# A state-space block with a feed-forward layer on one core: engine orders, scan steps, transfers and the PSUM ring re-ordered

## The reference, cut to what matters

```python
# x: 8 batches x 1024 tokens x 512, fp32
x = L0_attn_x
x = x + _layernorm(_L0_attn_ref(_layernorm(x), ...))
x = x + _layernorm(_L0_ffn_ref(_layernorm(x), ...))

# _L0_attn_ref
s = sigmoid(silu(x @ s_w1.T + s_b1) @ s_w2.T + s_b2)      # 512 -> 256 -> 128
u = (x @ B_w.T + B_b) * s
h = h @ A.T + u_t                                         # scan over 1024 tokens, state 128
y = hs @ C_w.T + C_b + x @ D_w.T + D_b
return y * sigmoid(x @ g_w.T + g_b)

# _L0_ffn_ref: a shared expert, and routed experts whose weight is trunc(softmax of two)
out_shared = square(relu(xf @ Ws1)) @ Ws2                 # 512 -> 256 -> 512
```

## Time and profile before

| | |
|---|---|
| median of 3 runs | 957.19 us (956.58 to 958.75) |
| the profiled execution | 963.26 us, span 961.5 us |
| TensorE busy, of the span | 91% |
| VectorE, GpSimd, ScalarE busy | 58%, 45%, 32% |
| mean granted clock of TensorE | 0.974 |
| moved by transfers | 72.9 MB |

### The profile page before, as it was taken

One profiled execution on the slowest core, in us unless ns is written; L12 is line 12 of the kernel. 1 busy time (PEld: TensorE's weight loads), 2 busy tenths in 40 slices (PEclk: granted clock), 3 DMA queues, 4 the chain that ended last, 5 costly groups with the idle time before them and its releaser, 6 DMA issues. The chain is left out here.

```text
span 961.5 us, 13116 instructions
## 1 busy us (share of the span) xinstructions
PE 873.0 (91%) x4120; PEld 712.5 (74%) x4120; DVE 559.8 (58%) x1392; ACT 310.2 (32%) x530; POOL 435.6 (45%) x537
## 2 busy tenths in 40 slices
PE   5689999999889998899998998899988999899975
PEld 4577877788767887678776887678876788787764
DVE  4826764577536675377744776367762767534652
ACT  3331433233322333224332243322342233322232
POOL 1342455254534446254552554444452545615454
PEclk9889999999999999999999999999999999999987
DMA  9030102321140111421023211402114110122112
GB/s 302 5 141 35 45 1 93 127 89 44 45 176 19 69 44 44 176 87 44 0 81 138 88 44 44 162 14 88 44 44 176 44 71 16 44 88 88 45 44 89
DMA packets 15129, 72.91 MB, mean 76 GB/s; under 512 B 2403, under 2 KB 4835, under 8 KB 7014
## 3 DMA queue, kind: packets, MB, share of 16 engines
q1 hardware_dynamic: 15078, 72.38, 19.9%
HBM read 38.82 MB, written 33.55 MB: 75 GB/s over the span
## 5 line engine op out<-in xcount | busy, mean ns | idle before, releaser
L415 PE MATMUL TM<-gw_hi,xT_hi 128*128 128x512 f32 x256 | 106.4, 416 | 0.9 <-ACT apt L766 0.7
L1399 POOL TENSOR_TENSOR rsv<-rsv,negh 128x1 f32<-128x1 f32 x64 | 35.9, 561 | 154.6 <-DVE rsv L1082 154.6
L415 PE MATMUL TM<-dw_hi,xT_hi 128*128 128x512 f32 x256 | 102.5, 400 | 0.0
L839 ACT ACTIVATE work<-TM,nmz,rsz 128x512 f32<-128x512 f32 x62 | 48.3, 779 | 164.3 <-POOL nmz L1409 164.3
L417 PE MATMUL TM<-gw_hi,xT_lo 128*128 128x512 f32 x256 | 100.8, 394 | 0.0
L417 PE MATMUL TM<-dw_hi,xT_lo 128*128 128x512 f32 x256 | 100.4, 392 | 0.0
L416 PE MATMUL TM<-gw_lo,xT_hi 128*128 128x512 f32 x256 | 100.0, 391 | 0.0
L416 PE MATMUL TM<-dw_lo,xT_hi 128*128 128x512 f32 x256 | 99.7, 390 | 0.0
L778 ACT ACTIVATE work<-TM 128x512 f32<-128x512 f32 x64 | 38.4, 600 | 171.5 <-PE TM L417 102.6
L1078 DVE TENSOR_TENSOR work<-TM,work 128x512 f32<-128x512 f32 x64 | 44.1, 689 | 81.8 <-PE TM L417 81.8
L1450 POOL TENSOR_TENSOR h_lo<-hf,h_hi 128x512 fp32r<-128x512 f32 x32 | 42.6, 1333 | 108.2 <-DVE h_hi L1140 108.2
(11 more groups left out here) (145 smaller groups left out, 2156.6 us busy)
## 6 DMA issues: line engine op xcount, KB each, us to landing
xin<-in_x SPq DMA_DIRECT2D x16, 1024.0 KB, 7.8
xres<-in_x SPq DMA_DIRECT2D x16, 1024.0 KB, 7.0
x_scratch<-xres SPq DMA_DIRECT2D x16, 1024.0 KB, 3.9
out<-work SPq DMA_DIRECT2D x15, 1024.0 KB, 4.8
xres<-in_g_w_t SPq DMA_DIRECT2D x1, 1024.0 KB, 7.7
xres<-in_D_w_t SPq DMA_DIRECT2D x1, 1024.0 KB, 7.5
work<-in_Ws SPq DMA_DIRECT2D x2, 512.0 KB, 9.2
out<-work SPq DMA_DIRECT2D x4, 256.0 KB, 2.0
```

The source lines that it names most:

```text
L415: eng.matmul(ps, lhs[0], rhs[0], start=first, stop=False)
L839: eng.activation(work[:, j, :], z_bank(rep, j)[:, :], ACT.Identity, bias=nmz[:, j:j + 1], scale=rsz[:, j:j + 1]).then_inc(S["zn_ok"], 1)
L1399: return eng.tensor_tensor(dst, src, negh[:, 0:n], ALU.pow)
```

## The change

The work is the same but for small pieces; its order changes on all engines. On TensorE, scan steps go between groups of three products of W1f and G, two groups apart; G(2) and G(3) move ahead in the tail, and the TM ring with them; in the body W1f(0,1) moves before Y(7), FT(5) before SG(0), W2(0) before T(4), H(1,0) and H(1,1) before W2(2) and W2(3). The other engines' orders follow. On VectorE the column of ones in xin is written once for four tiles. On SP the store of the result is issued in quarters of a batch (two tiles each, four semaphores), and xin is loaded two batches ahead, each half after the FT that reads the last tile of it, ahead of the store of x1. SP's loop has one pass less. Left out below: the two new semaphores and the waits at the very end.

```diff
--- before.py
+++ after.py
@@ -210,7 +211,7 @@
-        TM_RING = (3, ["g0", "g1", "z4", "z5", "g2", "z6", "z7", "g3", "y0", "g4", "y1", "g5", "y2", "g6", "y3", "g7",
+        TM_RING = (3, ["g0", "g1", "g2", "z4", "z5", "g3", "z6", "z7", "y0", "g4", "y1", "g5", "y2", "g6", "y3", "g7",
                        "y4", "y5", "y6", "y7", "z0", "z1", "z2", "z3"])
@@ -342,12 +343,16 @@
+            def store_out(b, h):
+                js = slice(2 * h, 2 * h + 2)
+                eng.wait_ge(S["out_ok"], body_at("out_ok", b, 2 * h + 1))
+                eng.dma_start(out_v[b][:, js, :], work[:, js, :]).then_inc(S[f"out_st{h}"], 16)
+            def load_next_x(n, m):
+                eng.wait_ge(S["ft_done"], prep_at("ft_done", n - 1, m * MS + MS - 1))
+                load_x(n, m)
             def one_pass(b, rep):
-                if rep + 1 < NB:
-                    eng.wait_ge(S["ft_done"], prep_at("ft_done", b, L - 1))
-                    for m in range(NM):
-                        load_x(b + 1, m)
                 if rep == 0:
@@ -355,25 +360,26 @@
                         if m == NM - 1:
-                            eng.wait_ge(S["out_ok"], body_at("out_ok", b - 1, L - 1))
-                            eng.dma_start(out_v[b - 1][:, js, :], work[:, js, :]).then_inc(S[f"out_st{m}"], 16)
+                            store_out(b - 1, 2)
+                            store_out(b - 1, 3)
                         eng.wait_ge(S["x1_st" + str(m)], body_at("x1_st" + str(m), b - 1))
-                        if m < NM - 1:
-                            eng.wait_ge(S["out_ok"], body_at("out_ok", b - 1, m * MS + MS - 1))
+                        eng.wait_ge(S["out_ok"], body_at("out_ok", b - 1, m * MS + MS - 1))
                     eng.dma_start(xres[:, js, :], x_v[b][:, js, :]).then_inc(S[f"xres_ld{m}"], 16)
...
                     js = slice(m * MS, (m + 1) * MS)
+                    if rep + 2 < NB:
+                        load_next_x(b + 2, m)
                     eng.wait_ge(S["x1_ok"], body_at("x1_ok", b, m * MS + MS - 1))
                     eng.dma_start(x1_v[b][:, js, :], xres[:, js, :]).then_inc(S[f"x1_st{m}"], 16)
-                for m in range(NM - 1):
-                    js = slice(m * MS, (m + 1) * MS)
-                    eng.wait_ge(S["out_ok"], body_at("out_ok", b, m * MS + MS - 1))
-                    eng.dma_start(out_v[b][:, js, :], work[:, js, :]).then_inc(S[f"out_st{m}"], 16)
+                store_out(b, 0)
+                store_out(b, 1)
+            for m in range(NM):
+                load_next_x(1, m)
             one_pass(0, 0)
-            with eng.Fori(1, NB - 1) as b:
+            with eng.Fori(1, NB - 2) as b:
                 one_pass(b, 1)
+            one_pass(NB - 2, NB - 2)
             one_pass(NB - 1, NB - 1)
@@ -491,7 +497,7 @@
-            def W1f(b, rep, m, f):
+            def W1f(b, rep, m, f, steps={}):
@@ -503,7 +509,10 @@
                             (x2T_hi[:, :, k, :], x2T_lo[:, :, k, :]), k == 0, k == KD - 1)
-                r.then_inc(S["w1_done"], 1)
+                    if k == KD - 1:
+                        r.then_inc(S["w1_done"], 1)
+                    if k in steps:
+                        scan_step(b, rep, steps[k])
@@ -575,22 +584,18 @@
                     return
-                G(*a, 0, {2: 0, 3: 1})
-                W1f(*a, 1, 0)
-                scan_step(*a, 2)
-                W1f(*a, 1, 1)
-                scan_step(*a, 3)
-                G(*a, 1, {2: 4, 3: 5})
-                scan_step(*a, 6)
+                G(*a, 0, {2: 0})
+                W1f(*a, 1, 0, {0: 1, 2: 2})
+                W1f(*a, 1, 1, {0: 3, 2: 4})
+                G(*a, 1, {0: 5, 2: 6})
+                G(*a, 2, {0: 7, 2: 8})
                 W2(*a, 4)
-                scan_step(*a, 7)
+                scan_step(*a, 9)
                 W2(*a, 5)
-                G(*a, 2, {2: 8, 3: 9})
+                scan_step(*a, 10)
+                G(*a, 3, {1: 11})
                 W2(*a, 6)
-                scan_step(*a, 10)
                 W2(*a, 7)
-                scan_step(*a, 11)
-                G(*a, 3)
@@ -623,30 +628,29 @@
                     B(*a, 0)
+                    FT(*a, 5)
                     SG(*a, 0)
                 Y(*a, 6)
-                if prep:
-                    FT(*a, 5)
                 W1f(*a, 0, 0)
-                Y(*a, 7)
-                if prep:
+                if prep:
+                    W1f(*a, 0, 1)
+                    Y(*a, 7)
                     FT(*a, 6)
-                if prep:
-                    W1f(*a, 0, 1)
                     FT(*a, 7)
+                    W2(*a, 0)
                     T(*a, 4)
-                    W2(*a, 0)
                     W2(*a, 1)
                     T(*a, 5)
+                    H(*a, 1, 0)
                     W2(*a, 2)
-                    H(*a, 1, 0)
                     T(*a, 6)
+                    H(*a, 1, 1)
                     W2(*a, 3)
-                    H(*a, 1, 1)
                     T(*a, 7)
...
                 else:
+                    Y(*a, 7)
                     W1f(*a, 0, 1)
@@ -767,10 +771,9 @@
                 eng.wait_ge(S["g_done"], body_at("g_done", b, j))
-                if j % MS == 0 and rep > 0:
-                    m = j // MS
-                    eng.wait_ge(S[f"out_st{m}"], body_at(f"out_st{m}", b - 1))
+                if j % 2 == 0 and rep > 0:
+                    eng.wait_ge(S[f"out_st{j // 2}"], body_at(f"out_st{j // 2}", b - 1))
                 elif rep == 0 and j in (0, 2, 3, 4):
@@ -847,17 +850,16 @@
                 gate(*a, 1)
+                gate(*a, 2)
+                hs(*a, 0)
                 if tail:
                     zn(*a, 4)
-                gate(*a, 2)
+                hs(*a, 1)
                 if tail:
                     zn(*a, 5)
-                hs(*a, 0)
-                hs(*a, 1)
+                gate(*a, 3)
                 if tail:
                     zn(*a, 6)
-                gate(*a, 3)
-                if tail:
                     zn(*a, 7)
@@ -894,16 +896,14 @@
                     ft_hi(*a, 4)
+                    ft_hi(*a, 5)
                     s_gate(*a, 0)
                 x1_norm(*a, 4)
-                if prep:
-                    ft_hi(*a, 5)
                 hidden(*a, 0, 0)
...
                 if prep:
+                    hidden(*a, 0, 1)
                     ft_hi(*a, 6)
-                if prep:
-                    hidden(*a, 0, 1)
                     ft_hi(*a, 7)
@@ -913,11 +913,11 @@
                     t_hi(*a, 6)
+                    sig(*a, 1, 1)
                     zn(*a, 2)
-                    sig(*a, 1, 1)
-                    zn(*a, 3)
                     t_hi(*a, 7)
                     s_gate(*a, 1)
+                    zn(*a, 3)
                 else:
@@ -1029,7 +1029,8 @@
                 eng.wait_ge(S["l1_rs"], prep_at("l1_rs", n, j // MS))
-                eng.memset(xin[:, j, 0:1], 1.0)
+                if j % MS == 0:
+                    eng.memset(xin[:, j:j + MS, 0:1], 1.0)
                 eng.tensor_scalar(xin[:, j, 1:D], xin[:, j, 1:D], mv1[:, j, 0:1], rs1[:, j:j + 1],
@@ -1165,45 +1166,46 @@
                 scan_add(*a, 0)
+                if prep:
+                    ln1_stats(b + 1, 0)
                 scan_add(*a, 1)
                 scan_add(*a, 2)
+                if prep:
+                    ln1_stats(b + 1, 1)
+                scan_add(*a, 3)
                 if tail:
                     h2(*a, 1, 0)
-                if prep:
-                    ln1_stats(b + 1, 0)
-                scan_add(*a, 3)
-                if prep:
-                    ln1_stats(b + 1, 1)
                 scan_add(*a, 4)
+                scan_add(*a, 5)
                 if tail:
                     h2(*a, 1, 1)
-                scan_add(*a, 5)
+                scan_add(*a, 6)
                 if prep:
                     ln1_stats(b + 1, 2)
-                scan_add(*a, 6)
+                scan_add(*a, 7)
                 if prep:
                     ln1_stats(b + 1, 3)
-                scan_add(*a, 7)
+                scan_add(*a, 8)
+                hs_low(*a, 0)
+                scan_add(*a, 9)
                 if tail:
                     z_stats(*a, 4)
-                if prep:
-                    ln1_stats(b + 1, 4)
-                scan_add(*a, 8)
+                scan_add(*a, 10)
+                hs_low(*a, 1)
                 if tail:
                     z_stats(*a, 5)
-                scan_add(*a, 9)
-                scan_add(*a, 10)
-                hs_low(*a, 0)
+                if prep:
+                    ln1_stats(b + 1, 4)
+                scan_add(*a, 11)
+                if prep:
+                    ln1_stats(b + 1, 5)
                 if tail:
                     z_stats(*a, 6)
-                scan_add(*a, 11)
-                hs_low(*a, 1)
-                if prep:
-                    ln1_stats(b + 1, 5)
+                if prep:
+                    ln1_stats(b + 1, 6)
```

(124 more changed lines are left out.)

## The result

The kernel after takes 934.50 us (932.95 to 936.70, four runs) against 957.58 for the kernel before beside it: ratio 0.9747, 95% interval 0.9727 to 0.9766. That is 23.1 us less; the forecast was 929, 28 less. The profiled execution took 932.95, span 931.2, against 963.26 and 961.5: 30.3 less.

What follows compares the result with a forecast made beforehand. TensorE, busy 873 of 961.5 us, was taken as the bound, leaving only its idle time and clock to win. Terms summed to -23.0, the clock -5, so -28: 957 - 28 = 929 us, range 916 to 950.

Steps and rivals of the forecast that it cites:

- A: FFN middle: W2(0) starts 2.81 us late after T(4), seven times, 19.7 in all; forecast to become 0.
- FT(5): FT(5) ahead of SG(0): waits uncovered for T(3)'s low part, 1.05 us lost a pass, +7.4 in seven passes.
- T(4): FFN middle: T(4) waits for its bank, freed by a low part behind attn(7) on VectorE; 0.7 lost a pass, +4.9.
- W2(7): Tail: W2(7) waits for z5's bank, loss 1.5 us a pass instead of 1.25; 1.2 of it idle.
- D: Tail: waits at the scan step of u, W2(4) and W2(7), 17.6 us in all, falling to 10.2.
- T(0): After the tail: VectorE's lag of some 1.3 us makes T(0) lose 0 to 1.1, taken as 0.4; +2.8 in all.
- B: Wait on the last low part of SG(1): 6.7 us over seven passes, forecast near 5.6, a gain of 1.1.
- C: Scan steps 1 and 2 after the loop's branch back: 12.1 us over five passes, forecast to fall to 0.5.
- the rival: Fetch gap stays before step 1: TensorE idles some 3 us in five passes, +15; 946 us, chance 0.2.
- I take its length as now: VectorE's wait of 4.9 us for code after the branch back was assumed to keep its length, despite fewer transfers in flight.
- The first pass: Steps close together and hs_low(0) behind gate(2) in the first pass: +1 us once.
- The clock: TensorE's clock granted at half after four waits, 7 us lost in all; forecast gain 5, bounds 0 and 7.

Runs made afterwards that it cites:

- The run with hs(1) moved: Kernel after, with ScalarE's hs(1) put ahead of zn(4) in the tail: 924.40 us, ratio 0.9617 to the kernel before.
- the FFN middle alone: Kernel before, with only the change's FFN middle orders on all engines, without FT(5)'s move, scan steps, memsets or SP's part: 929.65 us, ratio 0.9683.
- the transfers alone: Kernel before, with only SP's part of the change (early xin loads, output stored in quarters) and matching gate waits: ratio 1.0071.
- the 2 MB copy: Kernel after, its code moved back by 12 instructions, plus an unneeded 2 MB copy once a pass, some 3 us before the branch back: ratio 1.0268.
- 2 MB of loads ahead of it: Kernel before with the FFN middle orders, plus SP's two xin loads issued before the store of tiles 0 to 3, ahead of the branch: ratio 0.9955.

## Why the forecast came out 5 us low

**A** is gone whole, by the cover that was worked out: in the seven passes that prepare a batch W2(0) starts right behind FT(7).

**FT(5)** idles 0.98 for 1.05. Its price was a little over its term: taking it away gave 1.2 a pass, 8.4 for 7.4. **T(4)** idles 0.55 (0.5 to 0.7 forecast) and **W2(7)** 1.21 (1.2 forecast); the other two waits of **D** are gone. **T(0)** idles 0.53, more than the 0.4 lost that I took. **B** idles 6.2 in all for 5.6 in the kernel before: the small gain of 1.1 did not come. The run with hs(1) moved shows that what held W2(7) also made half of T(0)'s wait.

**C** is gone, to 0 (forecast 0.1 a pass), but my account of it held half of the cause. The shift by 12 instructions does what I said: alone it takes the gap away, and undone in the kernel after it costs 6 us (0.9809 less 0.9747, of 958), where the rival was given 15. The step that failed is "I take its length as now": with the queues empty the gap is 1.7 to 1.9 long, not 4.9. For the same reason no gap of 4 to 5 us shows at another instruction, as I had written that it would: the kernel after has none at all in its loop. And "step 0's own add, 1 us late" was the first block, fetched through the same burst: that add starts 2.0 behind the first instruction transfer and 1.0 behind TensorE's product, 0.2 behind the product in the kernel after. And the control that I named against traffic, pass 1 "which has the same transfers in flight", tells nothing about it: pass 1 has no branch back, so nothing to fetch. Code and traffic had to go wrong together for the 4.9, and the FFN middle alone undid the second.

**The last pass** was given no term for its orders. W2(0) idles 3.7 there for 2.6. attn_norm(7), put ahead of h2(0,1) on VectorE, is a likely cause: it waits for GpSimd, and h2(0,1) starts at 894.2, 1.4 behind the end of its input on ScalarE (892.8). It was not tried by itself. **The first pass** did not cost the 1 forecast: pass 0 is 0.7 shorter, about what A less FT(5) and T(4) gives, and the startup ahead of it 1.1, for which no run gives a cause.

**The clock** is the term that was mis-sized. Between the profiled executions the sum was near: -28 forecast, -30.3 measured, and no fall of the clock is left in passes 1 to 6, where four stretches of 3.4 us at half were (at 369.6, 482.2, 738.2 and 823.5; the prediction had 3.6 us each), 6.8 lost in all. The other 23.5 stand beside a sum of 23.0 without the clock; that this fits so well is in part luck, as FT(5), T(0), B and the last pass came out dearer and the start cheaper. Between the medians it is -23.1, again about the sum without its clock term. The step "as a difference, 957 - 28" took what a profiled execution lost and subtracted it from a median that had not lost it. The executions bear it out: those of the kernel before beside the experiments go from 958.04 at clock 0.983 to 963.95 at 0.974, the four after from 932.95 at 0.987 to 936.70 at 0.981. The profiled one of before, 963.26 at 0.974, lies at the slow end, that of after at the fast end. Which falls the other executions lack no trace shows, so this cause rests on the clocks alone.

**What the change left on the table**: of its parts the FFN middle alone gave 30 us. FT(5), hs(1) behind a norm and T(0) took back more than the tail gained.

## What to carry to other kernels

Behind a loop's branch back VectorE waited here for code, and longer with data under way than with the queues empty: look at which transfers SP issues in the few us before the branch, and move either them or the branch, and keep a dependent chain off the first instructions behind it. When a step is moved, ask of each instruction that it passes on every engine whether it is a short one behind a long one: a copy of 0.3 us behind a norm cost this kernel 10 us. Subtract a profile's stalls from that profile's own time, and compare its clock with the other executions' before carrying the sum to a median.

## What the runs showed of the hardware

Behind a branch back, the second instruction transfer on q14 came this long behind the first: 5.2 to 5.9 us in the kernel before, where SP issues 4 MB from 388.0 to 391.0; 5.9 to 7.3 in the run with the transfers alone (passes 3 to 6), where SP issues only 1.5 MB around it, so the amount does not decide alone; 4.6 to 4.7 with the 2 MB copy; 2.4 to 2.6 with the queues empty (kernel after, passes 3 to 6; the FFN middle alone 2.4). The first one came 0.3 to 0.5 us behind VectorE's last step of the pass with the queues empty (both, passes 3 to 6), 1.3 in the kernel before, 3.4 to 3.6 with 2 MB of loads ahead of it, and 5.8 to 6.1 with the copy (passes 3 to 6). In these two runs step 0's add waited 5.2 to 5.6 and 7.8 to 8.3 on issue. The Trainium skill's rule (Runtime: NRT & Kernel Launch, Instruction fetch mechanics), that a taken branch whose target is not in the fetched window has its page fetched before it goes on, agrees with these rows. That the time of the fetch hangs on what data is under way is what these runs add; by which part of the path the two meet, no run shows.
